# The 3x3 depthwise convolution of a two-branch image block: vector taps on one side, fp16 diagonal matmuls on the other

## The chip, the cores and the metric

The kernel runs on one core of a Trainium2 chip. The metric is device time in microseconds (us) of the whole launch, over all 32 images. Five engines work side by side, each with its own in-order queue and tied to the others by semaphores: TensorE (PE in the profile, its weight loads PEld), VectorE (DVE), ScalarE (ACT), GpSimd (POOL) and SyncE (SP). The on-chip memories are SBUF and, for what TensorE writes, PSUM.

## The reference, cut to what matters

The input `x` is 32 images of 56x56 pixels and 96 channels, float32. Two residual steps follow each other:

```python
x = x + L0(gn(x), W_v, W_a, b_a, W_o, b_o)   # local attention over 3x3 windows, stride 2, 12 heads
x = x + L1(gn(x), w)                         # 3x3 depthwise convolution

def gn(v, G=32, eps=1e-5):                   # per image: mean and variance over 56x56 pixels x 3 channels
    ...
    return ((g - m) / jnp.sqrt(s + eps)).reshape(v.shape)

def L1(x, w):                                # stride 1, zero rim, one 3x3 kernel per channel
    w_clip = jnp.clip(w, -1.0, 1.0)
    binary_kernel = w_clip + lax.stop_gradient(jnp.sign(w_clip) - w_clip)
    ...                                      # the weights are the signs, +1, 0 or -1
```

L0 makes values `v = x @ W_v` and logits from 2x2-pooled pixels (9x9 per head and window), takes the softmax, sums the values of a window with these weights, folds the windows back onto the image and multiplies by `W_o`. L1 is the part that the change rewrites: nine shifted copies of the normalised image, each times a sign per channel, added to the image itself.

## The kernel before

Channels lie on the 96 partitions, so an image is a tile of 96 x 3136 elements. One pass of the loop is called a body here. A body has 64 slots (`BODY`), 32 (`SLOTS`) for the upper half of the image and 32 for the lower. Three images are in flight: while body i runs the attention sums of image i (flag `s2`), image i+1's input, pooling, logits and softmax are prepared (flag `s1`), and the convolution and output of image i-1 are done (flag `cv`). The program runs body -1 (preparation alone), body 0 (attention sums and preparation, no convolution), a hardware loop over bodies 1 to 30, body 31 and body 32 (convolution alone, L251 to L256).

In every slot g the four engines pass one unit on. TensorE broadcasts two sets of softmax weights to the channels by fp16 matmuls into PSUM (`broadcast`, L733, tile `bc`, two buffers). VectorE multiplies them with the values (`product`, L600, tile `prod`, four buffers; reads `bc` in PSUM and `VAL` in SBUF). Where both terms belong to one output class, and the slot is in the list `PRE`, GpSimd adds the two halves (`pre_add`, L363); TensorE then multiplies by `W_o` and sums in PSUM (`add_up`, L753, tile `acc`), three slots later (`LAG`). So a slot in `PRE` costs one float32 matmul of 392 columns, another slot two; the profile shows a float32 matmul as two records. VectorE adds each finished class to `X1` (`add_class`, L611).

All other work is hung on slots by the table `AT`: it says after which slot's product, broadcast or pair addition a piece stands in its engine's queue. Side matmuls (values, logits, transposes in and out, group means: `fill_use`) go to two PSUM banks `side0` and `side1` in turn, each read by ScalarE before it is refilled (`read_use`). The softmax of image i+1 runs on GpSimd (subtract L345, multiply L351, second fp16 part L356), ScalarE and VectorE (`soft`: maximum L623, sum L627, reciprocal L631).

The convolution before: ScalarE copies `X1` to `ACC` and sums it (`start_acc`, L498), squares it (L506), writes the normalised, rimmed image to `XP` in float32 (`rimmed`, L527) and the centre tap into `ACC` (L534). VectorE then runs 24 taps (`tap`, L647): 8 positions x 3 row pieces of 1064, 1064 and 1008 elements, each `ACC = XP_shifted * sign + ACC`, with both tensors in SBUF. `AT["taps"]` puts one at slot 14, and the others at slots 17 to 53. After the last tap TensorE transposes `ACC` back (L710) and ScalarE stores it.

## Time and profile before

| quantity | value |
|---|---|
| device time, median of 3 runs | 5119.74 us (5117.42 to 5121.8) |
| profiled execution, span from first to last instruction | 5120.9 us |
| DVE busy | 4730.3 us, 92% |
| PE busy | 4119.3 us, 80% |
| POOL busy | 4037.2 us, 79% |
| ACT busy | 2005.6 us, 39% |
| granted TensorE clock, mean | 0.85 |

The profiled execution has no time of its own in the table of runs; its span lies inside the range of the three runs, so nothing that could be measured lies around it. Busy time of PE is modelled and counts a matmul from start to end, so that stretches with a lower granted clock look busier. Durations on the other engines are of single instructions. A body in the steady loop takes about 157 us; a head of 99 us stands ahead of body 0's first product and a tail of 60 us behind body 31's last. In the windows view a row gives a stretch, its length, the busy time of each engine with its number of instructions in it, the granted clock, the share of the DMA engines and GB/s. The windows below are cut at the starts of the products of slots 0, 12, 24, 36, 44 and 56 of a body.

### The profile page before, as it was taken

The numbers are of one execution on the slowest core, as the hardware profiler recorded it, in microseconds if no ns is written. First come the engines' busy times: TensorE is split into PE (matmuls) and PEld (weight loads), VectorE is DVE, ScalarE is ACT, GpSimd is POOL, SyncE is SP. The second block draws the span as 40 slices with busy tenths as digits, with TensorE's granted clock in tenths as the row PEclk, the third lists the DMA queues.
The fourth block names the chain that finished last, engine by engine and source line by source line (L and its number), as shares of the span: only waits on it lengthen the run. The fifth ranks groups of instructions, "written<-read, shape, count | busy, mean of one in ns | idle before, by whom it ended". The sixth has DMA issues, their size and how long they took to land.

```text
span 5120.9 us, 55367 instructions
## 1 busy us (share of the span) xinstructions
PE 4119.3 (80%) x13632; PEld 2114.1 (41%) x13632; DVE 4730.3 (92%) x3723; ACT 2005.6 (39%) x2753; POOL 4037.2 (79%) x3628
## 2 busy tenths in 40 slices
PE   4877887878887888878788887888878888878885
PEld 2434444434444344444344443444434444434442
DVE  5799999999999999999999999999999999999997
ACT  4424444334443344432444433444324444334431
POOL 5787877877877888778878788787787787887883
PEclk7988888888888788888888888888888888888887
DMA  1110111101111111111011111111110111111111
GB/s 39 38 38 24 47 44 37 47 21 40 47 33 47 36 25 47 42 39 47 21 40 47 33 47 30 31 47 38 43 47 15 46 47 33 47 24 37 47 29 28
DMA packets 126083, 194.36 MB, mean 38 GB/s; under 512 B 14248, under 2 KB 115464, under 8 KB 122472
## 3 DMA queue, kind: packets, MB, share of 16 engines
q1 hardware_dynamic: 97384, 155.50, 13.0%
q10 hardware_dynamic: 28672, 38.55, 2.5%
q8 instruction: 11, 0.18, 0.0%
q14 instruction: 16, 0.13, 0.0%
HBM read 39.22 MB, written 38.54 MB: 15 GB/s over the span
## 4 chain that ended last, share of the span: by engine, by line
POOL 45%; issue 25%; PE 18%; ACT 5%; DVE 5%; DMA 1%; SPq 0%; DVEq 0%; POOLq 0%; ACTq 0%; PEldq 0%; PEld 0%
POOL prod L363 15%; POOL part L356 10%; POOL att L351 10%; PE acc L753 10%; POOL att L345 6%; PE bc L733 4%; DVE prod L600 2%; ACT X L440 2%; POOL pc L332 2%; PE side L698 2%; ACT X L523 2%; PE side L692 1%; DVE ACC L647 1%; PE side L710 1%; DVE top L631 1%
## 5 line engine op out<-in xcount | busy, mean ns | idle before, releaser
L753 PE MATMUL acc<-prod,wo 96*96 96x392 f32 x5312 | 2478.5, 573 | 161.8 <-POOL prod L363 155.7
L600 DVE TENSOR_TENSOR prod<-bc,VAL 96x784 f32<-96x784 f32 x2048 | 1928.2, 959 | 307.5 <-PE bc L733 289.4
L363 POOL TENSOR_TENSOR prod<-prod 96x392 f32<-96x392 f32 x1440 | 1685.5, 1178 | 501.3 <-DVE prod L600 491.7
L733 PE MATMUL bc<-stack,sel 96*96 96x392 f16 x4608 | 1303.2, 378 | 633.5 <-DVE prod L600 611.5
L647 DVE SCALAR_TENSOR_TENSOR ACC<-XP,sg,ACC 96x1064 f32<-96x1064 f32 (+1 forms) x768 | 1736.2, 2281 | 14.9 <-ACT ACC L534 13.8
L753 PEld LDWEIGHTS acc<-prod,wo 96*96 96x96 f32 x5312 | 982.1, 188 | 675.1 <-issue 271.6
L733 PEld LDWEIGHTS bc<-stack,sel 96*96 96x96 f16 x4608 | 576.2, 137 | 1571.4 <-DVE prod L600 972.2
L351 POOL TENSOR_TENSOR att<-att,top 108x420 f32<-108x420 f32 (+1 forms) x576 | 750.3, 1321 | 38.3 <-ACT top L467 38.3
L345 POOL TENSOR_TENSOR att<-att,top 108x420 f32<-108x420 f32 (+1 forms) x576 | 645.1, 1138 | 144.2 <-DVE top L623 144.2
L356 POOL TENSOR_TENSOR part<-att,part 108x420 f16<-108x420 f32 (+1 forms) x576 | 737.3, 1298 | 0.0
L433 ACT ACTIVATE att<-side,ba 108x420 f32<-108x420 f32 (+1 forms) x576 | 340.5, 597 | 671.6 <-PE side L698 659.0
L698 PE MATMUL side<-pooled,wa 96*108 96x392 f32 (+1 forms) x1152 | 528.0, 573 | 46.3 <-ACT att L433 23.2
L627 DVE TENSOR_REDUCE top<-att 108x105 f32<-108x945 f32 (+1 forms) x256 | 456.9, 1796 | 14.5 <-ACT att L464 14.5
L623 DVE TENSOR_REDUCE top<-att 108x105 f32<-108x945 f32 (+1 forms) x256 | 449.3, 1786 | 15.4 <-ACTq L247 13.2
L426 ACT ACTIVATE VAL<-side 96x392 f32<-96x392 f32 (+1 forms) x256 | 124.7, 512 | 857.5 <-DVE prod L600 713.5
L475 ACT ACTIVATE part<-att 108x1260 f16<-108x1260 f32 (+1 forms) x192 | 234.5, 1221 | 470.4 <-POOL att L351 470.2
L698 PEld LDWEIGHTS side<-pooled,wa 96*108 96x108 f32 x1152 | 221.6, 197 | 305.4 <-issue 224.0
L446 ACT ACTIVATE tok_out<-side 112x384 f32<-112x384 f32 x224 | 110.2, 492 | 605.7 <-PE side L710 304.6
L464 ACT ACTIVATE att<-att 108x1260 f32<-108x1260 f32 (+1 forms) x192 | 232.4, 1210 | 140.5 <-POOL att L345 140.5
L692 PE MATMUL side<-XN,wv 96*96 96x392 f32 (+1 forms) x512 | 244.1, 573 | 7.8 <-ACT tok_out L446 3.8
L370 POOL TENSOR_TENSOR gve<-eps,gvar 96x1 f32<-96x1 f32 x64 | 13.2, 206 | 281.8 <-ACT spill L451 268.8
L440 ACT ACTIVATE X<-side 96x448 f32<-96x448 f32 x224 | 204.2, 1000 | 29.4 <-PE side L704 28.2
(55 smaller groups left out, 2183.7 us busy)
## 6 DMA issues: line engine op xcount, KB each, us to landing
stack<-part SPq DMA_DIRECT2D x192, 275.3 KB
stack<-part SPq DMA_DIRECT2D x192, 256.9 KB
tok_in<-in_x SPq DMA_DIRECT2D x32, 1176.0 KB, 9.7
out<-tok_out ACTq DMA_DIRECT2D x224, 168.0 KB, 4.2
stack<-part SPq DMA_DIRECT2D x192, 30.5 KB
stack<-part SPq DMA_DIRECT2D x192, 28.5 KB
X<-in_L_conv_W_a SPq DMA_DIRECT2D x1, 364.5 KB
ACC<-select SPq DMA_DIRECT2D x1, 144.0 KB
```

The source lines that it names most:

```text
L345: nc.gpsimd.tensor_tensor(att[h][:, k, :], att[h][:, k, :], top[h][:, :], ALU.subtract).then_inc(fine_step, 1)
L351: nc.gpsimd.tensor_tensor(att[h][:, k, :], att[h][:, k, :], top[h][:, :], ALU.mult).then_inc(fine_step, 1)
L356: nc.gpsimd.tensor_tensor(low, a4(h)[:, k], high, ALU.subtract).then_inc(fine_step, 1)
L363: nc.gpsimd.tensor_tensor(p[:, 0, :], p[:, 0, :], p[:, 1, :], ALU.add).then_inc(pre_added, 1)
L433: ins = nc.scalar.activation(att[h][:, k, :], bank[0:QN, 0:cols], ACT.Identity, bias=ba[:, k:k + 1])
L600: nc.vector.tensor_tensor(prod[:, g % PRODUCTS, :, :].rearrange("c a (i j) -> c a i j", j=WIN), b, v, ALU.mult).then_inc(prod_ready, 1)
L623: ins = nc.vector.tensor_reduce(top[h][:, c], by_window[:, c, :], AX.X, ALU.max)
L627: ins = nc.vector.tensor_reduce(top[h][:, c], by_window[:, c, :], AX.X, ALU.add)
L647: nc.vector.scalar_tensor_tensor(a, XP[:, r0 + ty:r1 + ty, tx:tx + SIDE], sg[:, t:t + 1], a, ALU.mult, ALU.add).then_inc(tapped, 1)
L698: last = nc.tensor.matmul(bank[0:QN, 0:ROWS[h] * WIN], wa[:, k, :, :], pooled[:, 0:ROWS[h], :], start=True, stop=True)
L733: last = nc.tensor.matmul(bc[g % 2][0:CH, a, 0:UNIT], sel[:, which, :], stack[h][:, qi, ki * TAPS + kj, si:si + HALF, sj:sj + WIN], start= ...
L753: last = nc.tensor.matmul(acc[c % 2][0:CH, 0:UNIT], wo[:, :], prod[:, g % PRODUCTS, a, :], start=first, stop=s == LAST[c] and (g in PRE or ...
```

## The change

The taps are gone from VectorE. The normalised image is held as two fp16 parts, `XP[0]` (the value rounded) and `XP[1]` (the rest), and nine diagonal matrices of the signs, `dg` (96x96, fp16), are made once at the start. TensorE computes the convolution in 7 strips of 8 rows (448 columns): 9 taps x 2 parts = 18 matmuls into one side bank, 9 in one slot and 9 in the next (`CONV_SLOTS`). VectorE adds each strip from PSUM to `ACC` (`add_conv`, L648).

Around it: `add_class` now also leaves its row sums (`accum_out`), so that the group mean no longer waits for the copy `start_acc`; that copy now waits for the mean and subtracts it. `rimmed` and the centre taps on ScalarE make way for `half` (three pieces, fp16), and VectorE makes the second part with three instructions (`rest`, L640, both tensors in SBUF). GpSimd loses four one-column operations and gets 54 pair additions in place of 45 (slots 3, 9, 10, 14, 15, 22, 33, 46 and 54 are new), and TensorE so nine float32 matmuls fewer. The values of the upper half move from slots 27, 30, 33, 33 to 32, 33, 33, 36.

```diff
-    "not pre": (0, 3, 8, 9, 10, 14, 15, 16, 22, 28, 33, 39, 46, 51, 54),
+    "not pre": (0, 8, 16, 28, 39, 51),
...
-    "taps": (14, 17, 18, 18, 19, 20, 20, 21, 25, 29, 30, 31, 32, 34, 35, 45, 48, 48, 48, 50, 50, 52, 53, 53),
+    "halved": (11, 11, 12),
+    "rest": (12, 13, 14),
+    CONV: (15, 24, 26, 28, 30, 34, 37),
+    "conv added": (18, 26, 28, 30, 32, 37, 39),
...
+STRIPS, STRIP = 7, SIDE // 7
+CONV_SLOTS = 2
...
-        XP = sb("XP", [CH, PAD_P, PAD_P])
+        XP = [sb(f"XP{p}", [CH, PAD_P, PAD_P], F16) for p in range(PARTS)]
...
             def start_acc(i):
 
-                until(act, y_added, upto(8, i, 0))
+                until(act, side_read, done(READS, i, GA, 1, 0))
                 nc.scalar.activation(ACC[:, :, :], X1[:, :, :], ACT.Identity,
-                                     accum_out=sums[:, 1, 0:1]).then_inc(acc_init, 1)
+                                     bias=nmean[:, 1:2]).then_inc(acc_init, 1)
...
-            def rimmed(i):
...
-            def centre_tap(i, part):
...
+            def half(i, part):
+                if part == 0:
+                    until(act, gn_scale, upto(6, i, 2))
+                r0, r1 = CUTS[part], CUTS[part + 1]
+                nc.scalar.activation(XP[0][:, 1 + r0:1 + r1, 1:1 + SIDE], ACC[:, r0:r1, :], ACT.Identity,
+                                     scale=rstd[:, 1:2]).then_inc(halved, 1)
...
+            for t in range(KK):
+                nc.vector.tensor_scalar(dg[:, t, :], idn[0:CH, 0:CH], sg[:, t:t + 1], None, ALU.mult).then_inc(
+                    weights_up, 1)
...
-                nc.vector.tensor_tensor(xv, acc[c % 2][0:CH, 0:UNIT].rearrange("c (i j) -> c i j", j=WIN), xv,
-                                        ALU.add).then_inc(y_added, 1)
+                n = 4 * h + c
+                nc.vector.scalar_tensor_tensor(xv, acc[c % 2][0:CH, 0:UNIT].rearrange("c (i j) -> c i j", j=WIN), 0.0,
+                                               xv, ALU.add, ALU.add, accum_out=sums[:, 1, n:n + 1]).then_inc(y_added, 1)
...
-                nc.vector.scalar_tensor_tensor(a, XP[:, r0 + ty:r1 + ty, tx:tx + SIDE], sg[:, t:t + 1], a,
-                                               ALU.mult, ALU.add).then_inc(tapped, 1)
+                nc.vector.scalar_tensor_tensor(XP[1][:, 1 + r0:1 + r1, 1:1 + SIDE], ACC[:, r0:r1, :], rstd[:, 1:2],
+                                               XP[0][:, 1 + r0:1 + r1, 1:1 + SIDE], ALU.mult,
+                                               ALU.subtract).then_inc(rest_ready, 1)
+
+            def add_conv(i, k):
+                n = next(n for n, u in enumerate(USES) if u[2] == CONV and u[4] == k)
+                until(dve, side_full, upto(len(USES), i, n + 1))
+                a = ACC[:, k * STRIP:(k + 1) * STRIP, :].rearrange("c h w -> c (h w)")
+                nc.vector.scalar_tensor_tensor(a, side[n % 2][0:CH, 0:STRIP * SIDE], nmean[:, 1:2], a, ALU.subtract,
+                                               ALU.add).then_inc(conv_added, 1)
...
+                m, ago = before_in_bank(n, True)
+                until(pe, conv_added, upto(STRIPS, i - ago, USES[m][4] + 1))
+                m, ago = before_in_bank(n, False)
+                until(pe, side_read, done(READS, i - ago - USES[m][1], *USES[m][2:]))
...
+            def conv(i, n, k, turn):
+
+                steps_of = [(t, p) for p in range(PARTS) for t in range(KK)]
+                per = len(steps_of) // CONV_SLOTS
+                if turn == 0:
+                    last_row = min((k + 1) * STRIP, SIDE - 1)
+                    until(pe, rest_ready, upto(3, i, next(c for c in range(3) if last_row < CUTS[c + 1]) + 1))
+                for m in range(turn * per, (turn + 1) * per):
+                    t, p = steps_of[m]
+                    ty, tx = divmod(t, TAPS)
+                    r = k * STRIP + ty
+                    ins = nc.tensor.matmul(side[n % 2][0:CH, 0:STRIP * SIDE], dg[:, t, :],
+                                           XP[p][:, r:r + STRIP, tx:tx + SIDE], start=m == 0,
+                                           stop=m == len(steps_of) - 1)
+                if turn == CONV_SLOTS - 1:
+                    ins.then_inc(side_full, 1)
```

How this stands in the queues is shown at two places. First TensorE in body 31, from the broadcast of slot 24 on (`bc` is a broadcast, `acc` the product with `W_o`, `side` a side bank). Before:

```order
L733 MATMUL bc0<-stack0,sel 96x392 x2
L753 MATMUL acc0<-prod,wo 96x392
L733 MATMUL bc1<-stack0,sel 96x392 x2
L753 MATMUL acc0<-prod,wo 96x392
L733 MATMUL bc0<-stack0,sel 96x392 x2
L753 MATMUL acc0<-prod,wo 96x392
```

The same place of the changed program:

```order
L742 MATMUL side1<-XP0,dg 96x448 x9
L757 MATMUL bc1<-stack0,sel 96x392 x2
L777 MATMUL acc0<-prod,wo 96x392
L742 MATMUL side1<-XP1,dg 96x448 x9
L757 MATMUL bc0<-stack0,sel 96x392 x2
L777 MATMUL acc0<-prod,wo 96x392
L742 MATMUL side0<-XP0,dg 96x448 x9
L757 MATMUL bc1<-stack0,sel 96x392 x2
L777 MATMUL acc0<-prod,wo 96x392
L742 MATMUL side0<-XP1,dg 96x448 x9
```

Between two broadcasts there now stand nine convolution matmuls in every one of the slots 24 to 31, where nothing but the slot's own matmuls stood.

Second VectorE in the steady loop, at slots 37 to 39 (`prod` is the slot's product, `top` the softmax sum; the register rows belong to the loop's counters). Before:

```order
L600 TENSOR_TENSOR prod<-bc,VAL 96x784
L627 TENSOR_REDUCE top<-att 108x105
L243 REGISTER_ALU
L600 TENSOR_TENSOR prod<-bc,VAL 96x784
L627 TENSOR_REDUCE top<-att 108x105
```

The same place of the changed program:

```order
L599 TENSOR_TENSOR prod<-bc,VAL 96x784
L628 TENSOR_REDUCE top<-att 108x105
L253 REGISTER_ALU
L648 SCALAR_TENSOR_TENSOR ACC<-side,nmean,ACC 96x448
L253 REGISTER_ALU
L599 TENSOR_TENSOR prod<-bc,VAL 96x784
L628 TENSOR_REDUCE top<-att 108x105
```

The addition of a convolution strip now stands behind the softmax sum of slot 37, and TensorE's refill of the same side bank, in its slot 37, waits for the strip added there (`conv_added`).

## Rows read from the trace of the kernel before

**Rows 1.** The page, busy time by engine: us, share of the span, instructions.

```profile
PE 4119.3 (80%) x13632; PEld 2114.1 (41%) x13632; DVE 4730.3 (92%) x3723; ACT 2005.6 (39%) x2753; POOL 4037.2 (79%) x3628
```

**Rows 2.** Windows, steady body: length, busy of PE, PEld, DVE, ACT, POOL; clock, DMA.

```profile
2582.86:2606.51 23.65, 21.66 (x103) 12.99 (x102) 20.75 (x19) 21.73 (x30) 14.65 (x20) 1.00 0.01 4
2606.51:2639.19 32.68, 26.81 (x80) 12.81 (x79) 31.66 (x24) 19.38 (x27) 28.36 (x26) 0.84 0.03 7
2639.19:2671.83 32.64, 25.68 (x72) 11.64 (x70) 32.01 (x27) 6.85 (x8) 29.19 (x24) 0.84 0.21 47
2671.83:2689.07 17.24, 14.50 (x42) 7.46 (x43) 17.03 (x15) 2.78 (x5) 10.42 (x10) 0.80 0.00 0
2689.07:2722.12 33.05, 24.87 (x71) 11.78 (x69) 32.95 (x24) 8.02 (x11) 30.21 (x23) 0.74 0.12 28
2722.12:2740.28 18.16, 16.67 (x65) 10.09 (x64) 14.49 (x14) 3.69 (x8) 13.88 (x15) 0.81 0.69 177
sum 157.42, PE 130.18 PEld 66.77 DVE 148.88 ACT 62.45 POOL 126.71; mean PE 21.70 PEld 11.13 DVE 24.81 ACT 10.41 POOL 21.12
```

**Rows 3.** The waits of the whole span: us in total, times, longest us.

```profile
PEld bc L733 <- DVE prod L600: 972.2, 661, 7.3
```

**Rows 4.** The windows view, body 0 (no convolution), cut at the same products.

```profile
99.37:124.25 24.88, 22.94 (x94) 12.88 (x93) 20.16 (x19) 12.73 (x19) 11.68 (x11) 0.89 0.10 28
124.25:145.68 21.43, 21.28 (x79) 11.46 (x78) 12.29 (x15) 15.29 (x23) 20.55 (x25) 1.00 0.00 1
145.68:168.81 23.13, 19.90 (x65) 9.76 (x64) 19.34 (x19) 5.22 (x8) 19.02 (x20) 0.93 0.34 76
168.81:188.15 19.34, 16.08 (x51) 8.05 (x50) 16.87 (x15) 4.68 (x6) 12.51 (x13) 0.82 0.00 1
188.15:212.84 24.69, 21.21 (x66) 10.40 (x65) 12.26 (x15) 7.52 (x10) 23.94 (x25) 0.86 0.16 39
212.84:231.22 18.38, 14.47 (x41) 6.60 (x40) 14.47 (x15) 0.71 (x2) 11.96 (x13) 0.81 0.46 118
sum 131.85, PE 115.88 PEld 59.15 DVE 95.40 ACT 46.15 POOL 99.65; mean PE 19.31 PEld 9.86 DVE 15.90 ACT 7.69 POOL 16.61
```

**Rows 5.** One line's instructions, in turn of L647, L363 and L600: ns min/median/max.

```profile
L647 DVE SCALAR_TENSOR_TENSOR ACC<-XP,sg,ACC x768: 1247/2004/6940, 257.4 to 5107.4; 96x1064 f32<-96x1064 f32 x128, 96x1008 f32<-96x1008 f32 x64
...
L363 POOL TENSOR_TENSOR prod<-prod x1440: 998/1016/2104, 101.3 to 5061.3; 96x392 f32<-96x392 f32 x180
...
L600 DVE TENSOR_TENSOR prod<-bc,VAL x2048: 898/959/1001, 99.4 to 5060.3; 96x784 f32<-96x784 f32 x187
```

**Rows 6.** Groups by shape: busy us, mean ns of one, idle before.

```profile
L647 DVE SCALAR_TENSOR_TENSOR ACC<-XP,sg,ACC 96x1064 f32<-96x1064 f32 x512 | 1222.0, 2388 | 14.6 <-ACT ACC L534 13.8 <-DVE ACC L647 0.8
L647 DVE SCALAR_TENSOR_TENSOR ACC<-XP,sg,ACC 96x1008 f32<-96x1008 f32 x256 | 529.0, 2067 | 0.2 <-DVE ACC L647 0.2
L611 DVE TENSOR_TENSOR X<-acc,X 96x392 f32<-96x392 f32 x256 | 141.1, 551 | 11.2 <-PE acc L753 11.0
...
L733 PEld LDWEIGHTS bc<-stack,sel 96*96 96x96 f16 x4608 | 576.2, 137 | 1571.4 <-DVE prod L600 972.2 <-issue 551.2 <-DMA stack<-part 16.6
...
L440 ACT ACTIVATION_READ_ACCUMULATOR X<-side 96x1 f32 x224 | 50.3, 225 | 0.0
```

**Rows 7.** TensorE in order of time, two slots: start us, us, engine line, count.

```profile
2602.45 0.51 PE L733 MATMUL bc<-stack,sel 96*96 96x392 f16 x2
2602.80 1.48 PE L753 MATMUL acc<-prod,wo 96*96 96x392 f32 x4
2604.11 0.51 PE L733 MATMUL bc<-stack,sel 96*96 96x392 f16 x2
```

**Rows 8.** The windows view, body 31 up to the end of its last product.

```profile
4937.96:5061.28 123.32, 103.57 (x345) 51.44 (x344) 110.40 (x102) 27.57 (x30) 83.96 (x74) 0.85 0.10 25
```

**Rows 9.** The tail in order of time: start us, us, engine line, count.

```profile
5063.60 0.56 DVE L611 TENSOR_TENSOR X<-acc,X 96x392 f32<-96x392 f32 x1 [1.88 <-PE acc L753]
...
5108.83 3.30 PE L710 MATMUL side<-idn,ACC 96*112 96x96 f32 x16 [37.07 <-DVE ACC L647]
```

More of the change, by code:

```diff
@@ L47 @@
 PART_UP = 4096.0
-V, LOG, IN, OUT, GA, GB = "values", "logits", "in", "out", "mean", "variance"
+V, LOG, IN, OUT, GA, GB, CONV = "values", "logits", "in", "out", "mean", "variance", "conv"
 MAX, SUM, INV = "maximum", "sum", "inverse"
@@ L102 @@
 USES = sorted(pieces(V, LOG) + [(at, 0, kind, g, 0) for kind in (GA, GB) for g, at in enumerate(AT[kind])]
[L103 to L104 removed]
+              + [(at, 0, kind, 0, n) for kind in (IN, OUT, CONV) for n, at in enumerate(AT[kind])],
+              key=lambda p: p[0])
+READS = [u for u in USES if u[2] != CONV]
+assert not any(at < u[0] < at + CONV_SLOTS for at in AT[CONV] for u in USES)
 SOFT = pieces(MAX, SUM, INV)
@@ L118, in upto, with before_in_bank @@
     return (i + 1) * per_body + n
+def before_in_bank(n, conv):
+    of = [m for m, u in enumerate(USES) if m % 2 == n % 2 and (u[2] == CONV) == conv]
+    now = [m for m in of if m < n]
+    return (now[-1], 0) if now else (of[-1], 1)
 def build_program(nc, x, W_v, W_a, b_a, W_o, b_o, w_conv, ident, group, select, out):
@@ L146, in build_program @@
         quarter = sb("quarter", [CH, 1])
-        one = sb("one", [CH, 1])
-        centre = sb("centre", [CH, 3])
+        dg = sb("dg", [CH, KK, CH], F16)
         tok_in = sb("tok_in", [TP, TT, CH])
@@ L227, in use_on @@
             _, late, kind, which, _ = use
-            if kind == OUT or (kind in (GA, GB) and which == 1):
+            if kind in (OUT, CONV) or (kind in (GA, GB) and which == 1):
                 return cv
@@ L540, in body @@
                         (AT["squares"][1], square_1, (i,), gn_square, cv),
-                         *((at, centre_tap, (i, n), centred, cv) for n, at in enumerate(AT["centred"])),
-                         (AT["rimmed"], rimmed, (i,), xp_ready, cv),
+                         *((at, half, (i, n), halved, cv) for n, at in enumerate(AT["halved"])),
                          *((AT["pool normed"][h], pool_norm, (i, h), pool_normed, s1) for h in range(2))]
@@ L654, in body @@
                 plan = [(at, soft, (i - late, *what), soft_step, s2 if late else s1) for at, late, *what in SOFT]
-                plan += [(at, tap, (i, n), tapped, cv) for n, at in enumerate(AT["taps"])]
+                plan += [(at, rest, (i, n), rest_ready, cv) for n, at in enumerate(AT["rest"])]
+                plan += [(at, add_conv, (i, n), conv_added, cv) for n, at in enumerate(AT["conv added"])]
                 for g in range(BODY):
```

127 lines of the change are left out of this document (54 added, 73 removed).

## The prediction

> **What bounds the kernel now.** I read the busy line of the page first [rows 1]: DVE leads with 92%, PE and POOL follow with 80% and 79%. A share over the whole span does not say which engine decides, so next the windows of one steady body, cut into six stages which I call A (slots 0 to 11), B (12 to 23), C (24 to 35), D (36 to 43), E (44 to 55) and F (56 to 63) [rows 2]. The reader is to see that DVE is busy for 31.66 of 32.68 us in B, 32.01 of 32.64 in C, 17.03 of 17.24 in D and 32.95 of 33.05 in E: in these four VectorE alone sets the time. In A and F it isn't full (20.75 of 23.65, 14.49 of 18.16). The waits agree [rows 3]: PE's broadcasts wait 972.2 us in all for DVE's products. 24 taps stand in a body: 1222.0 + 529.0 us of busy time over 32 images [rows 6] is 54.7 us of each image's DVE time, and they lie in B, C and E.
>
> The best witness for what is left when they go is in the same trace. Body 0 runs attention and preparation and no convolution, and takes 131.85 us [rows 4], with DVE busy for 95.40 and POOL for 99.65. So no engine is near full, and still it takes 131.85: a broadcast, a product, a pair addition and a product with `W_o` hand over to each other with two and four buffers, and an engine that is full in one stage cannot be relieved by another stage's idle time. In B and E POOL is full (20.55 of 21.43, 23.94 of 24.69), in C, D and F it is DVE with its softmax reductions, or the hand-over. I sum by stages for that reason.
>
> A steady body: 5061.28 is the end of the window of body 31 and 123.32 its length [rows 8]; from 231.22, where body 0 ends, to 4937.96 lie 30 bodies, 156.9 us each. The sum below is made against the profile's span of 5120.9 us, which lies in the range of the three runs, 1.2 us above their median.
>
> **The change part by part, prices first.** A convolution matmul is fp16, 448 columns. Two fp16 broadcasts of 392 columns start at 2602.45 and what follows at 2602.80 [rows 7]: 0.175 us each, scaled by 448/392 0.20 us; 18 x 7 = 126 of them are 25.2 us per image on PE. At the lower of the two clock levels it would be 0.40, the bound above; below, nothing suggests less than a column's time. A float32 product with `W_o` is two records, and four take 1.31 us (2602.80 to 2604.11 [rows 7]), so 0.655 us for each of the nine that go.
>
> That spacing holds with another weight load ahead of each matmul. The Trainium skill, "TensorE: Matmul & The Clock Gate", Measured speedup vs the span model, says that a weight load overlaps running matmuls only when it goes to other rows of the array; by that rule 126 loads would come on top. The rows speak against it, since a load of 137 ns [rows 6] would leave 38 of the 175 ns for 392 columns; its outcome is a rival below.
>
> `rest` is three instructions with two SBUF tensors of the taps' shapes. A tap takes 1247 ns at least and 2388 on average [rows 5, 6], and POOL's pair addition 1016 in the median and 2104 at most, while the product, with one operand in PSUM, stays between 898 and 1001. So two-SBUF-operand work on VectorE and GpSimd's work slow each other. I take 2.0 us for each (bounds 1.25 and 2.4), 6 us per image, and for POOL up to 3 us more; for all other POOL work the slowing goes with the taps. A strip's addition reads PSUM like L611, 551 ns for 392 elements [rows 6]: 0.63 for 448, 4.4 us per image (at the product's rate, 959 ns for 784, it would be 0.55).
>
> `add_class` now writes its row sums. No row of before shows that on VectorE; the nearest is ScalarE's reading of an accumulator, 225 ns [rows 6]. Bounds are 0 and 8 x 0.225 = 1.8 us per image; I take 1, as part of the stages' margins. The Trainium skill, "VectorE: DVE Perf Modes", Two Vector instructions with no wait between them, says that an operation that writes out its accumulator is two instructions; it gives no price, and no run here shows it yet.
>
> ScalarE swaps `rimmed` and the centre taps for `half`, 3 us less; it is 62.45 of 157.42 us busy, and hides that. GpSimd's four one-column operations are worth 0.7 us. The nine `dg` instructions at the start lie in the 99 us before the first product.
>
> **Stage by stage.** A stage takes what its fullest engine takes, and the hand-overs.
>
> A: steady 23.65, ScalarE 21.73 busy there [rows 2]. The copy to `ACC` now waits for the group mean (a matmul and two short ScalarE steps, under 1 us), and three pair additions come to POOL, 14.65 us busy. I take 24.5 (23.7 to 26).
>
> B: body 0 has 21.43. `rest` adds about 5 on VectorE, which is idle for part of that; a strip of 3.6 us and its addition come too, and the logits of slot 19 wait for the strip's addition at slot 18. POOL, full there, gets three pair additions. I take 28 (26.4 to 30).
>
> C: this is where TensorE becomes the bound. Its work by count: 24 broadcasts x 0.175 = 4.2, 14 products x 0.655 = 9.2, three value pieces about 0.7 each = 2.1, 90 convolution matmuls x 0.20 = 18.0: together 33.5 us, against 23.13 that body 0 took and 32.64 of today. Broadcasts may run two slots ahead, so that some 2 us can slip out at the ends. I take 32.5 (31.5 to 34.5): no gain at all in the stage.
>
> D: steady 17.24, body 0 19.34. Two additions are 1.3 us. Behind TensorE's waiting refill in slot 37 stands the broadcast of slot 38: it waits for product 37, the softmax sum behind it and the strip's addition, and then nine matmuls, 1.8 us, run while VectorE has no product; the same wait stands in slot 39. I take 20.5 (18.5 to 23).
>
> E: 24.69 in body 0, POOL full from its softmax multiplications and second parts; two pair additions more (slots 46 and 54), 1 us each. I take 26.5 (24.7 to 28).
>
> F: 18.38 and 18.16, unchanged: 18.3 (18.2 to 19).
>
> The sum is 24.5 + 28 + 32.5 + 20.5 + 26.5 + 18.3 = 150.3 us (lower bounds 143.0, upper 160.5). So of 54.7 us of taps 6.6 are left as gain: B gives 4.7, E 6.5, C nothing, D takes 3.3, A and F 1 together (the rounding is the body's, 157.4 against 156.9). Thirty bodies give 30 x 6.6 = 198 us. Body 0 gets nine pair additions, +4. Body 31 has little preparation; what B and E gain there, C gives back: 0. The tail from the last class addition to the first transposition is 45 us now (5064.2 to 5108.83 [rows 9]), 24 taps of about 1.25 us in it; with 25.2 us of matmuls and shorter ScalarE steps about 40, -5. In all 5120.9 - 199 = 4922 us.
>
> **The rivals.** *The busiest engine alone decides.* For it: in the steady body DVE reaches 148.88 of 157.42, 95%. The fullest engine would then be TensorE: by the prices above 18.6 + 23.8 + 33.5 + 16.5 + 17.6 + 12.6 = 122.6 us, at 95% 129, which gives 5120.9 - 30 x 28 = 4280. Against it: body 0, where the fullest did not reach 80%. The weaker form, that every stage comes out at its lower bound, gives 143.0 and 5120.9 - 30 x 13.9 = 4704.
>
> *TensorE's clock: slower than before.* In C the granted clock is 0.84 now, a third of the stage at the lower level (1.2 against 2.4 GHz), behind waits for products of up to 7.3 us [rows 2, 3]. If it stays at 0.84 where TensorE is the bound, C costs 33.5 / 0.84 = 39.9 in place of 32.5, and the body 157.7; with B's 23.8 us at 0.84 (28.3) 158.0: 5120.9 + 30 x 1.1 - 1 = 5153. It decides from a grant of 0.85 in C down. Against it: TensorE would have no long wait in C, and body 0 shows 0.93 there and 1.00 in B.
>
> *Hand-overs.* Each of the seven strips is added by VectorE before its bank is refilled. If each of these waits costs 1.5 us beyond what I put in, the body is at 157 to 161, the change gives nothing, and the time is 5120 to 5230. For it: the queue at slot 37. Against it: the other fills stand two slots or more behind the addition.
>
> *Weight loads in the open*: a load for a broadcast is 137 ns on average [rows 6]. Of the strips' 126 loads 108 lie in C and D, where they would be on the path: +15 us, 165, and 5360. Against it is the spacing of 0.175. This is what the Trainium skill's rule would give.
>
> **How the numbers follow.** Forecast by stages, 143 to 157 us a body: 0.78, 4922. Every stage at its lower bound or better (4704 and below): 0.11. Clock: 0.06. Hand-overs: 0.04. Loads: 0.01. The likeliest's own range is 4704 to about 5110. For 8 in 10 I take 4730 to 5075. Three runs differ by 0.09%, so 0.2% (10 us) is what tells a change from none. Of the hand-over case 0.01 is faster, 0.02 same and 0.01 slower. Faster by more: 0.78 + 0.11 + 0.01 = 0.90; same 0.02; slower 0.06 + 0.01 + 0.01 = 0.08.
>
> **What would show it.** In the changed profile: no DVE group of 54.7 us a body, DVE busy near 107 us of it; pair additions at 1.02 us with few of 2 us; stage C with PE filled and clock near 1.00, and of about the old length; D longer than now; E with POOL full. Strips' matmuls 0.19 to 0.20 us apart. It is wrong if C is much shorter than 31 us, or if convolution matmuls stand further apart than 0.2 us, or if B or E don't shrink.

## The result and the profile after

| | before | after |
|---|---|---|
| median | 5120.71 us (5117.42 to 5121.8, 4 runs) | 5478.26 us (5474.7 to 5479.01, 4 runs) |
| ratio | | 1.070, 95% interval 1.068 to 1.071 |

The kernel is 7% slower; 4922 us had been forecast, in a range up to 5075. The page of the changed kernel, in the form of [rows 1], busy us and share of the span:

```profile
span 5476.9 us, 63082 instructions
PE 4611.4 (84%) x17088; PEld 2566.8 (47%) x17088; DVE 3492.6 (64%) x3541; ACT 1908.6 (35%) x2689; POOL 3695.9 (67%) x3787
```

VectorE gave up 1240 us of work (4730.3 to 3492.6) and the launch still became longer: no engine is fuller than PE's 84%. So the time must be in waits. The windows of one steady body, cut at the same six places as [rows 2]:

```profile
2784.37:2813.64 29.27, 24.48 (x96) 15.16 (x95) 20.97 (x20) 21.60 (x30) 15.43 (x17) 0.77 0.00 0
2813.64:2843.66 30.02, 27.23 (x95) 14.28 (x94) 20.43 (x21) 16.35 (x25) 28.17 (x30) 0.89 0.00 0
2843.66:2876.40 32.74, 32.74 (x149) 19.50 (x148) 21.77 (x25) 3.08 (x5) 25.63 (x26) 1.00 0.24 54
2876.40:2908.64 32.24, 21.93 (x70) 11.44 (x69) 18.46 (x17) 6.77 (x8) 8.28 (x9) 0.79 0.00 0
2908.64:2933.59 24.95, 20.78 (x69) 10.40 (x67) 12.30 (x17) 7.81 (x11) 24.21 (x25) 0.86 0.16 37
2933.59:2951.63 18.04, 16.09 (x63) 9.47 (x62) 14.54 (x16) 3.94 (x9) 13.59 (x15) 0.81 0.71 186
sum 167.26, PE 143.23 PEld 80.24 DVE 108.47 ACT 59.55 POOL 115.30; mean PE 23.87 PEld 13.37 DVE 18.08 ACT 9.93 POOL 19.22
```

Row 3 (stage C) is full of TensorE at clock 1.00, as forecast. Row 4 (stage D) is the surprise: 32.24 us where [rows 2] has 17.24, and no engine is busy for more than 22 of them. Row 1 (stage A) is 5.6 us longer than before, at a clock of 0.77 in place of 1.00 (0.96 on average over the steady bodies before). Means over the steady bodies, the same cuts in every kernel:

| | head | body 0 | steady | A | B | C | D | E | F | body 31 | tail |
|---|---|---|---|---|---|---|---|---|---|---|---|
| before | 99.4 | 131.8 | 156.9 | 23.7 | 32.4 | 32.6 | 17.0 | 33.0 | 18.1 | 123.3 | 59.6 |
| forecast | 99.4 | 135.8 | 150.3 | 24.5 | 28 | 32.5 | 20.5 | 26.5 | 18.3 | 123.3 | 54.6 |
| after | 128.5 | 146.9 | 167.3 | 29.3 | 30.0 | 32.7 | 32.2 | 25.0 | 18.0 | 125.5 | 58.2 |

After less before is 29 (head) + 15 (body 0) + 30 x 10.4 + 2 - 1, about 356 us. After less forecast is 556 us: 510 of it in the steady bodies, of which D 11.7 x 30 = 351, A 4.8 x 30 = 144, B 60, and E 45 the other way; 29 in the head, 11 in body 0, 6 at the end.

The waits over the whole span (total us, times, longest us):

```profile
DVE prod L599 <- PE bc L757: 1698.5, 1145, 6.7
PEld side L742 <- DVE ACC L648: 272.6, 34, 8.9
PE side L742 <- DVE ACC L648: 250.9, 34, 8.2
DVE top L628 <- ACT att L465: 159.8, 32, 11.5
PE side L711 <- ACT X L441: 144.9, 63, 4.1
```

In [rows 3] TensorE waited for VectorE's products; now VectorE waits 1698.5 us for TensorE's broadcasts. The second and third row are rare and long, once a body: a strip's first matmul (L742) waits 8 us for VectorE's addition of an earlier strip (L648). The fourth row has nearly the same count (32), and is the link before it: VectorE's softmax sum waits for ScalarE's exponential. Stage D in order of time (start us, us, engine line, what; in brackets the idle time before):

```profile
2876.86 0.82 PE L699 MATMUL side<-XN,wv 96*96 96x392 f32 x2
...
2877.72 0.50 ACT L427 ACTIVATE VAL<-side 96x392 f32<-96x392 f32 x1 [5.48 <-PE side L699]
...
2878.11 1.24 ACT L465 ACTIVATE att<-att 108x1260 f32<-108x1260 f32 x1
...
2879.25 1.73 ACT L486 ACTIVATE XN<-X,shift,rstd 96x1624 f32<-96x1624 f32 x1
2880.88 1.24 ACT L465 ACTIVATE att<-att 108x1260 f32<-108x1260 f32 x1
...
2882.15 1.83 DVE L628 TENSOR_REDUCE top<-att 108x105 f32<-108x945 f32 x1 [4.78 <-ACT att L465]
2883.90 0.96 DVE L599 TENSOR_TENSOR prod<-bc,VAL 96x784 f32<-96x784 f32 x1
2884.78 1.83 DVE L628 TENSOR_REDUCE top<-att 108x105 f32<-108x945 f32 x1
2886.53 0.68 DVE L648 SCALAR_TENSOR_TENSOR ACC<-side,nmean,ACC 96x448 f32<-96x448 f32 x1
2887.26 0.23 PEld L742 LDWEIGHTS side<-XP,dg 96*96 96x96 f16 x2 [8.89 <-DVE ACC L648]
2887.26 3.60 PE L742 MATMUL side<-XP,dg 96*96 96x448 f16 x9 [8.23 <-DVE ACC L648]
...
2892.20 0.97 DVE L599 TENSOR_TENSOR prod<-bc,VAL 96x784 f32<-96x784 f32 x1 [5.00 <-PE bc L757]
```

The reader is to see one chain through three in-order queues. The last value piece comes out of TensorE at the end of the full stage C, and ScalarE, which reads it, has stood idle for 5.48 us with two exponentials and the normalisation queued behind. The softmax sum of slot 36 waits for the second of these exponentials (2880.88); behind it stand product 37, another sum, and only then the strip's addition, which frees the bank for which TensorE waits. TensorE idles 8.23 us, its clock falls (nine matmuls take 3.60 us here, 1.92 at 2893.26), and behind the strip wait the broadcasts.

### The profile page after: what moved, and what is told of

Read it like the earlier page. It is cut to its first block, busy times and chain, and to the rows that moved or that the text cites. A ratio compares the mean times of both kernels' runs of the same rounds, so it can differ in the third digit from the quotient of the medians.

```text
span 5476.9 us, 63082 instructions
## 1 busy us (share of the span) xinstructions
PE 4611.4 (84%) x17088; PEld 2566.8 (47%) x17088; DVE 3492.6 (64%) x3541; ACT 1908.6 (35%) x2689; POOL 3695.9 (67%) x3787
## 4 chain that ended last, share of the span: by engine, by line
POOL 49%; issue 35%; PE 7%; ACT 5%; DVE 1%; POOLq 1%; DVEq 1%; SPq 0%; PEldq 0%; DMA 0%; PEld 0%; ACTq 0%
POOL prod L372 22%; POOL att L354 9%; POOL att L360 9%; POOL part L365 8%; PE acc L777 3%; POOL pc L341 2%; ACT ACC L499 2%; ACT X L523 2%; PE bc L757 2%; PE side L711 1%; ACT X L441 1%; ACT XP L506 1%; DVEq L257 1%; POOLq L253 1%; PE side L742 0%
## 5 line engine op out<-in xcount | busy, mean ns | idle before, releaser
L599 DVE TENSOR_TENSOR prod<-bc,VAL 96x784 f32<-96x784 f32 x2048 | 1969.3, 966 | 1718.7 <-PE bc L757 1698.5
L372 POOL TENSOR_TENSOR prod<-prod 96x392 f32<-96x392 f32 x1728 | 1773.5, 1034 | 1266.2 <-DVE prod L599 1257.6
L777 PE MATMUL acc<-prod,wo 96*96 96x392 f32 x4736 | 2198.6, 561 | 183.8 <-POOL prod L372 181.5
L742 PE MATMUL side<-XP,dg 96*96 96x448 f16 x4032 | 938.2, 382 | 254.8 <-DVE ACC L648 250.9
L777 PEld LDWEIGHTS acc<-prod,wo 96*96 96x96 f32 x4736 | 859.3, 185 | 553.8 <-POOL prod L372 259.0
L742 PEld LDWEIGHTS side<-XP,dg 96*96 96x96 f16 x4032 | 535.0, 134 | 715.1 <-DVE ACC L648 272.6
L354 POOL TENSOR_TENSOR att<-att,top 108x420 f32<-108x420 f32 (+1 forms) x576 | 593.2, 1046 | 181.2 <-DVE top L624 181.2
L360 POOL TENSOR_TENSOR att<-att,top 108x420 f32<-108x420 f32 (+1 forms) x576 | 658.5, 1155 | 42.1 <-ACT top L468 42.1
L427 ACT ACTIVATE VAL<-side 96x392 f32<-96x392 f32 (+1 forms) x256 | 128.5, 514 | 1171.9 <-PE side L699 1057.0
L365 POOL TENSOR_TENSOR part<-att,part 108x420 f16<-108x420 f32 (+1 forms) x576 | 526.7, 933 | 0.0
L711 PE MATMUL side<-idn,tok_in 112*96 112x112 f32 x896 | 181.6, 356 | 189.2 <-ACT X L441 144.9
L711 PEld LDWEIGHTS side<-idn,tok_in 112*96 112x96 f32 x896 | 138.7, 178 | 283.2 <-ACT X L441 200.6
## 6 DMA issues: line engine op xcount, KB each, us to landing
stack<-part SPq DMA_DIRECT2D x192, 28.5 KB
```

Of the source, the lines that this page charges most:

```text
L354: nc.gpsimd.tensor_tensor(att[h][:, k, :], att[h][:, k, :], top[h][:, :], ALU.subtract).then_inc(fine_step, 1)
L360: nc.gpsimd.tensor_tensor(att[h][:, k, :], att[h][:, k, :], top[h][:, :], ALU.mult).then_inc(fine_step, 1)
L365: nc.gpsimd.tensor_tensor(low, a4(h)[:, k], high, ALU.subtract).then_inc(fine_step, 1)
L372: nc.gpsimd.tensor_tensor(p[:, 0, :], p[:, 0, :], p[:, 1, :], ALU.add).then_inc(pre_added, 1)
L599: nc.vector.tensor_tensor(prod[:, g % PRODUCTS, :, :].rearrange("c a (i j) -> c a i j", j=WIN), b, v, ALU.mult).then_inc(prod_ready, 1)
L711: last = nc.tensor.transpose(bank[0:CH, t * TP:(t + 1) * TP], tok_in[:, 4 * k + t, :], idn[:, :])
```

## The experiments

Each time stands beside runs of the kernel before on the same chip.

**The two links of stage D, one at a time and together.**

```diff
# e2_exp
-    EXP: ((33, 36, 37), (64, 65, 67)),
+    EXP: ((33, 35, 35), (64, 65, 67)),
# e3_add: add_conv stands first in VectorE's plan (ahead of the softmax steps of its slot), and
-    "conv added": (18, 26, 28, 30, 32, 37, 39),
+    "conv added": (18, 26, 28, 30, 32, 36, 39),
# e4_both: both
```

> Changed kernel with the second and third exponential moved from slots 36 and 37 to slot 35 of ScalarE's queue, ahead of the read of the last value piece (slot 36) and of the second normalisation. Theory E: stage D (now 32.2 us) is long because the softmax sum of slot 36 waits 4.8 us for these exponentials, which queue behind a read whose matmul stands in TensorE's slot 36; everything behind the sum, the strip's addition and TensorE's refill moves with it. Then the sum's wait goes, stage D falls by about 5 to 27, a body to 162, the time to about 5320. Rival H (the hand-over alone): the refill still waits for product 37, two sums and the addition, stage D falls by less than 2 us.

> Changed kernel with the addition of the sixth strip moved from behind the softmax sum of slot 37 to slot 36, ahead of the sum there. Theory H: TensorE's 8.2 us of idleness in slot 37 end with this addition; with it gone TensorE issues the strip and the broadcast of slot 38 under the sums, the 5.0 us wait of product 38 goes too and the clock stays up: stage D from 32.2 to about 24, the time to about 5240. Theory E: DVE's first wait, for the exponentials, stays (4.8 us), so stage D falls by no more than 5 or 6 us in all, to 26 to 27.

> The edits of e2_exp and e3_add together. If the two waits stand one behind the other, both gains add up: stage D at 20 to 22 us, which is what the forecast had, a body at 155 to 157, the time 5110 to 5180. If they are two views of one wait, it is no better than the better of the two.

Measured: e2_exp 5267.75 us, ratio 1.028 (1.025 to 1.031); e3_add 5266.84, 1.028 (1.025 to 1.031); e4_both 5056.56, 0.987 (0.984 to 0.990). Each alone takes 211 us off, together 422, as expected of two waits in a row on one chain. The gains themselves were larger than I had put them: e4_both was expected at 5110 to 5180, and e2_exp at about 5320. Stage D in e3_add lies between the 24 us of theory H and the 26 to 27 of theory E. The steady body goes 167.3, 160.4, 160.4, 153.6; stage D 32.2, 26.1, 25.2, 18.0. The second edit shortens D by 0.9 us more than the first, and yet both bodies are 160.43 us; so the equal gains are not the lengths of the two waits (see "Still open"). Stage D in e2_exp, e3_add and e4_both, in the same columns as above:

```profile
2768.14:2794.25 26.11, 20.64 (x70) 10.95 (x69) 18.41 (x16) 4.61 (x6) 8.29 (x9) 0.87 0.00 0
```

```profile
2770.24:2795.42 25.18, 20.23 (x70) 10.73 (x69) 18.30 (x17) 6.77 (x8) 8.28 (x9) 0.86 0.00 0
```

```profile
2662.01:2680.06 18.05, 17.13 (x70) 9.57 (x69) 18.05 (x17) 4.61 (x6) 8.23 (x9) 1.00 0.00 0
```

In e4_both VectorE is busy for all of the 18.05 us and TensorE for 17.13, at clock 1.00. The same operations in another order turn the change from 7% slower to 1.3% faster.

**ScalarE's copy ahead of its exponential (e5_acc)**, on top of e4_both: in `more`, `start_acc` first.

```diff
-                more = [(at, smooth, ...) for at, late, *what in SMOOTH]
+                more = [(AT["start acc"], start_acc, (i,), acc_init, cv)]
+                more += [(at, smooth, ...) for at, late, *what in SMOOTH]
```

> e4_both with the copy start_acc ahead of the exponential in slot 3 of ScalarE's queue. Theory A: stage A (29.3 us against 23.7 before) is long because the copy starts 8.3 us after product 0 instead of 4.1, so that the reads of the incoming image and with them TensorE's transpositions in slot 7 come late, TensorE stands 4.1 us and its clock drops; the copy now starts about 2 us earlier, TensorE's wait falls by as much and less of the stage is at the lower clock: stage A 26 to 27.5, a body near 151, the time 4970 to 5010. Rival: the exponential behind the copy now delays the softmax sum of slot 6 by 2.9 us and gives it back: A stays within 1 us of 29.3, time within 30 us of 5056.

Measured: 4958.61 us, ratio 0.968 (0.965 to 0.971), 98 us under e4_both. The copy starts 6.2 us after product 0 in place of 8.3 (before: 4.1); TensorE's wait behind it falls from 4.12 to 2.96 us. A goes 29.3 to 28.2, B 30.1 to 28.5, and D stays. I had expected the gain in A (26 to 27.5); most of it came in B. Stages A and B of a steady body:

```profile
2519.40:2547.68 28.28, 24.66 (x94) 15.26 (x93) 21.18 (x21) 21.70 (x30) 15.48 (x18) 0.76 0.00 1
2547.68:2576.05 28.37, 25.34 (x96) 12.97 (x95) 20.16 (x21) 16.16 (x25) 28.13 (x30) 1.00 0.00 0
```

The clock still falls in A, at slot 7. The changed kernel's second fall, at slot 13, is gone, so that all of B runs at 1.00, against 0.89 there.

**The kernel before's 45 pair additions in place of 54 (e6_pre45)**, on top of e4_both: its "not pre" line.

> e4_both with the 45 pair additions of before in place of 54: nine fewer on GpSimd, nine float32 matmuls (0.655 us each) more on TensorE. If GpSimd is the bound in B and E (as in body 0 of before), these shorten by about 1 us each and the time falls by 30 to 60 us. If TensorE matters more (full in C, at half clock in A), a body gets 1 to 4 us longer: 5090 to 5180.

Measured: 5006.14 us, ratio 0.977 (0.974 to 0.980), 50 us under e4_both: B -1.8 us, E -1.0, C +0.7. Here the nine additional pair additions cost more than the nine float32 products that they save. But B's part comes with the same thing as in e5_acc: the clock's fall at slot 13 is gone. Stage B:

```profile
2564.09:2592.34 28.25, 26.75 (x104) 14.56 (x103) 18.70 (x22) 16.58 (x25) 25.96 (x27) 1.00 0.00 0
```

**Two matmuls for a strip in place of eighteen (e7_twomm)**, on top of e4_both; 16 of 18 products are left out of each strip's sum.

> e4_both with two matmuls in each strip instead of 18 (16 of the 18 products of each strip are left out). Theory: TensorE's 24.2 us of strips (126 x 0.192) set stage C alone: C falls from 32.7 to 23 to 26, where VectorE's reductions and the hand-over rule, B by 1 to 2, the others by nothing: a body 143 to 146, the time 4730 to 4820. Rival: all 24.2 - 2.7 us are on the path, a body 132, 4400.

Measured: 4815.76 us, ratio 0.940 (0.937 to 0.943). 112 matmuls of 0.19 us, 21.5 us a body, are gone, and the body is 6.8 us shorter (146.8, where 143 to 146 was expected): C -7.4, B -1.5, D +2.7. Stage C:

```profile
2522.94:2548.26 25.32, 22.46 (x69) 11.19 (x68) 21.38 (x25) 4.17 (x6) 22.15 (x23) 0.80 0.31 69
```

With the matmuls gone TensorE's clock is 0.80 in C and 0.92 in D, against 1.00 in e4_both, which takes back part of the gain, by an amount that no run separates. Body 31 and the tail, in which convolution has little beside it, give 15 and 20 us.

**The kernel before with taps of one row (e8_thin)**: each of the 24 taps works on 56 elements, the rest of the convolution is left out.

> The kernel before with each of the 24 taps cut to one of its 19 or 18 rows (the convolution's other rows are left out): same instructions and waits, no tap time and little traffic. Hand-over theory of the forecast (body 0: 131.85 us with no engine over 76%): a body near 133 to 137, the time 4400 to 4520. Rival, the fullest engine decides (GpSimd, then TensorE, about 107 us): a body 112 to 118, the time 3700 to 3900.

Measured: 4371.26 and 4471.02 us, too far apart for a ratio; the first lies below the 4400 to 4520 that I expected, and the profile is of the slower one. The steady body is 136.5 us there, against 131.8 of body 0; 100 us less over 30 bodies make it an estimated 133 in the other run. So a body whose taps have little to do comes near body 0, and the rival (112 to 118) is out. But the removal wasn't clean:

```profile
L647 DVE SCALAR_TENSOR_TENSOR ACC<-XP,sg,ACC 96x56 f32<-96x56 f32 x768 | 897.4, 1189 | 16.9 <-ACT ACC L534 15.9 <-DVE ACC L647 1.0
```

One row still takes 1189 ns on average, half of a whole tap's 2388 [rows 6]: what is left isn't work on elements but a wait inside the instruction. Stage B is 29.9 us there and VectorE busy for 23 of it.

**The head (e1_head)**, on the changed kernel: TensorE's and GpSimd's start waits shortened, TensorE's full ones moved ahead of body 0.

```diff
-            pe.wait_ge(weights_up, N_UP)
-            pe.wait_ge(rims_zero, 4)
+            pe.wait_ge(weights_up, 2)
...
+                if s2 and not cv:
+                    pe.wait_ge(weights_up, N_UP)
+                    pe.wait_ge(rims_zero, 4)
```

> Changed kernel at 5478 us; only the waits at the start of TensorE's and GpSimd's queues are as before, and TensorE's wait for the diagonal matrices and the cleared rims stands ahead of body 0. Theory: the first transposition waited 42.8 us for the last dg instruction, and the first product came at 128.5 in place of 99.4 us, so the first product comes back to 99 to 101 us and the time to about 5449 (-29). Rival: the head is set by something else (the softmax of body -1, or the changed slots of values and normalisation), and the time stays within 5 us of 5478. Bodies keep 167.25 us in both.

Measured: 5460.4 us, ratio 1.066 (1.063 to 1.069); the first product comes at 111.5 us in place of 128.5, not at 99. TensorE's largest waits up to there, in the changed kernel and then in e1_head:

```profile
PE side L711 <- DVE dg L585: 42.8, 1, 42.8
```

```profile
PE side L704 <- DVEq L257: 17.4, 2, 13.7
```

The second one is a wait for VectorE's queue: `fill_use` has a new wait on `conv_added`, which in body -1 only counts skipped additions, and VectorE comes to those skips after its set-up. My theory covered 17 of the 29 us.

**All of it together (e9_best)**, with that wait left out in the two bodies before the loop; then **the square a slot later (e10_sq7)** and **`rest` on one row (e11_thinrest)**.

```diff
# e9_best: e4_both, e5_acc, e6_pre45, e1_head, and
-                until(pe, conv_added, upto(STRIPS, i - ago, USES[m][4] + 1))
+                if not (isinstance(i, int) and i <= 0):
+                    until(pe, conv_added, upto(STRIPS, i - ago, USES[m][4] + 1))
# e10_sq7: e9_best and
-    "squares": (13, 6),
+    "squares": (13, 7),
# e11_thinrest: e9_best, rest's three pieces with ACC[:, r0:r0 + 1, :] in place of ACC[:, r0:r1, :]
```

> The edits that helped so far, put together: V(0) exponentials at slots 33, 35, 35, strip additions ahead of the softmax steps with the sixth at slot 36, ScalarE's copy of y ahead of its exponential, the 45 pair additions of the kernel before in place of 54, TensorE's and GpSimd's start waits cut down, and one thing new: the added wait of TensorE for strip additions is left out in the two bodies before the loop, where no strip is filled. If the pieces add up: 4959 us of the run with the copy first, less 50 us (5057 less 5006, the pair additions), less the head. If those added waits tied TensorE to VectorE's set-up work in the body before the loop (it waited 13.7 us there with the start waits cut), the first product comes at 99 to 102 us and the time is about 4880 us (4870 to 4895). If VectorE's own set-up is the reason, the head stays at 111 us and the time is about 4892 us. If the pair additions and the copy remove the same wait, it is 4925 or more.

> The same, with ScalarE's square of the depthwise input back at slot 7, behind its reads of the first three input transpositions (the changed kernel has it at slot 6, ahead of two of them). Theory: in stage A (slots 0 to 11) TensorE stands behind the transpositions whose banks ScalarE reads late, because copy and square come first; with the square later TensorE's wait of about 3 us in slot 7 goes, its clock doesn't fall, and stage A goes from 28 to 25 or 26 us: 60 to 90 us less. Rival: the wait is for the copy, which starts 6 us after product 0 in either; then the square's place moves stage A by under 0.5 us, and, being later, it delays the variance and so stage B by up to 1 us: -15 to +30 us.

> The first of these three with each of VectorE's three instructions that make the second part of the split working on one row only (the rest of the second part is left out, so the sum of the convolution is not the reference's). They took 3.2 to 3.5 us twice and 1.25 us once an image; now about 0.1 us each, so 7.5 us of VectorE's work go. Theory one, they stand on the path of stage B (between the halved part and the first strip): stage B falls from 28 to 22 or 24 us, near body 0's 21 to 25: 120 to 200 us less. Rival: stage B is set by ScalarE's copy, square, normalisation and halving before them (with one-row taps the kernel before still took 29.9 us there): stage B falls by 1 to 2 us: 30 to 60 us less.

Measured: e9_best 4926.69 us, ratio 0.962 (0.960 to 0.964): the fastest complete kernel, with e10_sq7 (4925.22, 0.961, 0.960 to 0.963) level with it. e11_thinrest 4924.02. The first product is at 100.2 us in place of 111.5; e4_both's edits alone take 1.6 us off the head (128.5 to 126.9), so that about 10 to 11 of the 11.3 us are the added wait. But the body is 150.3 us as in e5_acc: the pair additions' 1.6 us are not there a second time, and the sum that I expected (4880) is missed by 47 us. The last of the three outcomes written down came true, "If the pair additions and the copy remove the same wait, it is 4925 or more". The windows show what they share: each of e5_acc and e6_pre45 brings B from 0.89 to 1.00, and that can be had only once. What is e6_pre45's own recurs, E -0.9 and C +0.7 against e5_acc. Stages A, B and C of e9_best, and the sum of the body:

```profile
2488.24:2516.33 28.09, 23.78 (x96) 14.83 (x95) 21.08 (x20) 21.50 (x30) 13.21 (x14) 0.82 0.01 3
2516.33:2544.57 28.24, 26.99 (x104) 14.68 (x103) 18.69 (x21) 16.57 (x25) 25.95 (x27) 1.00 0.00 0
2544.57:2577.97 33.40, 33.40 (x151) 19.82 (x150) 21.76 (x25) 5.47 (x7) 23.19 (x24) 1.00 0.24 53
...
sum 150.29, PE 139.45 PEld 79.73 DVE 106.47 ACT 59.35 POOL 106.77; mean PE 23.24 PEld 13.29 DVE 17.74 ACT 9.89 POOL 17.80
```

TensorE is now busy for 139.45 of 150.29 us. In e10_sq7 A falls by 1.4 us, and B, E and F rise by as much; in e11_thinrest B falls by 1.6, and A, E and F rise (body 150.2). My theory fell in both. Of the rivals, e10_sq7's held for the time, though A moved by more than its 0.5 us; e11_thinrest's held for stage B (1 to 2 us), but not for the time: 2.7 us less in place of 30 to 60.

**TensorE's input transpositions later (e12_in)**, on top of e9_best. What it is aimed at is TensorE's two idle times in stage A of e9_best:

```profile
2502.48 0.59 PE L712 MATMUL side<-idn,tok_in 112*96 112x112 f32 x4 [2.30 <-ACT X L441]
...
2506.09 0.98 PE L712 MATMUL side<-idn,tok_in 112*96 112x112 f32 x4 [2.01 <-ACT X L441]
```

```diff
-    IN: (5, 7, 7, 8, 9, 10, 10),
+    IN: (6, 8, 9, 10, 10, 11, 11),
-    GB: (17, 9),
+    GB: (17, 10),
```

> The version of the best run with TensorE's seven input transpositions at slots 6, 8, 9, 10, 10, 11, 11 in place of 5, 7, 7, 8, 9, 10, 10, and the sum of squares' small product at slot 10 in place of 9. In the best run TensorE stands 2.3 and 2.0 us in stage A for ScalarE's reads of the second and third transposition, behind ScalarE's copy of y (2.9 us), an exponential, the new residual (2.9) and the square (2.8), and from there it runs 13.7 us at half clock. Theory: given other products first, TensorE has no wait there, the clock stays up, and stage A goes from 28.2 to 24.5 to 26 us, which was the forecast for it; stage B may give back 1 us, since the input's sums come later. That is 50 to 110 us: 4820 to 4880. Rival: ScalarE is the bound of this stretch (21.5 us busy of 28) and the reads end as late as before; what A gains B loses, or a wait for the broadcasts at half clock takes its place; the steady body stays at 150.2 us as in the last four kernels and the time at 4920 to 4930.

Measured: 4957.18 us, ratio 0.970 (0.966 to 0.974), runs from 4939 to 4985. A falls to 24.4 on average, the forecast's number, and B rises to 31.6: my theory for the time fell, and what A gained B lost, as the rival said; the time is 30 us above e9_best, which neither had. In one of the 30 steady bodies the clock stays up through A and B, and it takes 146.7 us:

```profile
2499.96:2523.82 23.86, 21.43 (x101) 12.69 (x100) 20.81 (x20) 19.77 (x29) 12.02 (x15) 1.00 0.00 0
2523.82:2552.12 28.30, 25.66 (x100) 13.95 (x99) 18.79 (x22) 17.95 (x26) 27.08 (x28) 1.00 0.00 0
```

In six it falls once, at slot 13, and they take 150.0 us; in the other 23 it falls at slot 9 or 10 and again at 13, and they take 149.7 to 156.8. So the forecast for A and B (52.5 us together) was met in one body (52.2), and not held.

## Why the prediction was wrong, point by point

**Stage D, 20.5 forecast, 32.2 measured: the step that failed**, 351 of 556 us. The prediction put it as "Behind TensorE's waiting refill in slot 37 stands the broadcast of slot 38: it waits for product 37, the softmax sum behind it and the strip's addition". It named the right queue, and priced what stands in it, but not how late its first member comes. The softmax sum waits for an exponential on ScalarE, and that for a value piece that the change had moved to TensorE's slot 36, behind the 90 strip matmuls of stage C, and for a normalisation moved between two exponentials. ScalarE was dismissed with "62.45 of 157.42 us busy, and hides that". e2_exp and e3_add show it: with one link out 211 us come back, with both 422, and D is 18.0, 2.5 less than forecast.

**Stage A, 24.5 forecast, 29.3 measured**, 144 us. The failed step: "The copy to `ACC` now waits for the group mean (a matmul and two short ScalarE steps, under 1 us)". The mean is short, but the copy was moved behind it in ScalarE's queue, and so behind an exponential too:

```profile
2792.65 2.90 ACT L499 ACTIVATE ACC<-X,nmean 96x3136 f32<-96x3136 f32 x1
...
2795.66 2.91 ACT L523 ACTIVATE X<-X,bo 96x3136 f32<-96x3136 f32 x1
...
2798.74 0.97 ACT L441 ACTIVATE X<-side 96x448 f32<-96x448 f32 x1 [0.17 <-ACT X L523]
...
2799.77 0.98 PE L711 MATMUL side<-idn,tok_in 112*96 112x112 f32 x4 [4.12 <-ACT X L441]
```

It starts 8.3 us after product 0 (2784.37), not 4.1; two operations of 2.9 us run before ScalarE reads the first transposition, and TensorE, which needs that bank, idles 4.12 us. Its clock falls within that time, to a mean of 0.77 in the stage, and a transposition's four matmuls take 0.98 us behind it, against 0.55 ahead of it. e5_acc takes 98 us of A and B back, e12_in brings A to 24.4.

**Stage B, 28 forecast, 30.0 measured.** The base, body 0's 21.43, has nothing of the chain that feeds the convolution: copy, square, normalisation, halving on ScalarE. `rest` was taken at 2.0 us each; the row of the changed kernel, min/median/max ns, and its shapes (busy us, mean ns):

```profile
L640 DVE SCALAR_TENSOR_TENSOR XP<-ACC,rstd,XP x96: 1254/3146/3495, 305.5 to 5434.1; 96x1064 f16<-96x1064 f32 x64, 96x1008 f16<-96x1008 f32 x32
...
L640 DVE SCALAR_TENSOR_TENSOR XP<-ACC,rstd,XP 96x1064 f16<-96x1064 f32 x64 | 204.6, 3199 | 10.0 <-ACT XP L529 10.0
```

So two of the three took 3.2 us on average, above my upper bound of 2.4. Yet e11_thinrest, without that work, takes 1.6 us off B and nothing off e9_best's body. 1.6 of B's 2.0 us over the forecast go when the clock's fall at slot 13 does (0.89 to 1.00 in e5_acc, B 28.5).

**Pair additions.** Three a stage were counted as filling POOL in A and B and two in E, at 1 us each; nine fewer gave 50 us in e6_pre45's comparison, and nothing in e9_best's steady body against e5_acc's. E's 0.9 to 1.0 us is there both times, and C loses 0.7 for it. That they are slower beside two-operand VectorE work was right: of the 1440 of before 230 took over 1.2 us (mean 1178 ns), with the taps gone 31 of 1728 (mean 1034).

**The head, 0 forecast, +29 measured.** "The nine `dg` instructions at the start lie in the 99 us before the first product": they do, but TensorE's first instruction waits for the last of them, 42.8 us. 17 of the 29 us are this wait (e1_head), 10 to 11 the new waits in body -1 (e9_best, back at 100.2). Body 0's 11 us over the forecast go with the two links of stage D: it is 136.1 in e4_both, where 135.8 was forecast.

**What was right.** Strip matmuls 0.20 us apart. A row of nine, and the row of the eight weight loads between them:

```profile
2893.26 1.92 PE L742 MATMUL side<-XP,dg 96*96 96x448 f16 x9
2893.26 1.49 PEld L742 LDWEIGHTS side<-XP,dg 96*96 96x96 f16 x8 [0.45 <-issue]
```

Eight loads in 1.49 us, the last 0.12 long, are 0.196 us apart, and so are the matmuls: the loads aren't in the open, and that rival is out. The rule of the Trainium skill that it went by stands in "TensorE: Matmul & The Clock Gate" under The mechanism, not under the section that the prediction names; these rows, whose loads all go to the same 96 rows of the array, don't bear it out. Stage C 32.7 us with TensorE full at clock 1.00 (32.5 forecast, clock rival out), E 25.0 in its range, F 18.0 just under its 18.2 to 19; e7_twomm confirms that C is set by those matmuls. A strip's addition took 671 ns (630), and the accumulator's read on VectorE has a row now, 78 ns, so 0.6 us an image of the 0 to 1.8:

```profile
L648 DVE SCALAR_TENSOR_TENSOR ACC<-side,nmean,ACC 96x448 f32<-96x448 f32 x224 | 150.3, 671 | 24.8 <-PEq L257 14.8 <-PE side L742 9.7
...
L612 DVE DVE_READ_ACCUMULATOR X<-acc,X 96x1 f32 x256 | 20.1, 78 | 0.0
```

The rival of the hand-overs put a slower kernel at the right place, slot 37, but at 1.5 us for each of seven waits; it was one wait, of 12 us with what follows from it. The time measured lies above all the rivals' too: none of them had the queues of ScalarE.

**Still open.** e5_acc, e9_best, e10_sq7 and e11_thinrest all have a mean steady body of 150.2 to 150.3 us, with stages that differ by up to 2 us; e2_exp and e3_add both have 160.43. TensorE is busy for 136.8 us of a body in e5_acc, 139.5 in e9_best and 141.9 in e11_thinrest. The granted clock says more. In the changed kernel it changes twelve times in each of bodies 2 to 30, at the same twelve points of the body to 0.03 us, and those bodies are 167.22 to 167.27 us long; e1_head, e2_exp, e3_add, e7_twomm and e11_thinrest repeat as closely, to 0.1 us. In e9_best and e10_sq7 single bodies take 148.8 to 152.9 us, and only the mean is 150.3. e12_in adds that without the fall in A alone nothing is gained (150.0 us, clock 1.00 in A, a fall at slot 13), and that without any in A and B a body takes 146.7. So a body's length seems tied to where the clock changes, and a gain in one stage can be lost in the next for that reason; no run here isolates it. The 211 us of each link are then what the whole program gained, and not the length of a wait.

## What to carry to other kernels

When an operation is moved from one engine to another, follow every queue that the moved pieces pass, not only the two engines: what cost 422 us here was the order of three short instructions on an engine that was 35% busy, and of one addition on an engine that was 64% busy. For a wait that is added, ask when the first member of the queue ahead of it can start, back through each engine, and not only how long its members take; and where a wait serves only the loop, look at what it couples in the prologue. A change that loses by such an order is worth keeping for the next try: with the order alone mended (e5_acc) it is 3.2% faster than before, with the start waits and pair additions too (e9_best) 3.8%.
